# A graph network on one core: masks behind the picks, row numbers once a turn, and one arrival count for eight tiles

## What is computed

```python
def spmm(h):
    msg = h[src] * edge_w[:, None]
    agg = jax.ops.segment_sum(msg, dst, num_segments=N)
    return agg + self_w[:, None] * h
h = relu(batchnorm(spmm(x @ W1 + b1)))
x = layernorm(x + spmm(h @ W2 + b2))
# second layer: attention along the edges, softmax over edges of the same src ("row")
scores = (q[row] . k[col]) / sqrt(16) + edge_emb @ eb_w.T + eb_b
attn = softmax of scores over the edges of a row
out = segment_sum(attn * v[col], row);  x = layernorm(x + out @ out_w.T + out_b)
```

## Time and profile before

| | |
|---|---|
| median of 3 runs | 9340.04 us |
| profiled execution | 9334.91 us, its span 9333.3 us |
| mean granted TensorE clock | 0.796 of full |
| busy: TensorE matmul, weight load | 6708.6 us (72%), 5384.7 us (58%) |
| busy: VectorE, POOL, ScalarE | 5772.2 us (62%), 6065.1 us (65%), 2627.6 us (28%) |
| stretches in steady state | first product 600 to 2200 us, second product 2800 to 5200 us, expansion 5600 to 7400 us |

### The profile page before, as it was taken

How to read it: one execution, slowest core, us unless ns; L and a number is a source line. 1 busy time by engine, 2 the same in 40 slices (tenths; PEclk the granted TensorE clock), 3 DMA queues, 4 the chain that set the end, 5 groups by cost and what they waited for, 6 DMA issues and landing times. The chain is left out here.

```text
span 9333.3 us, 196145 instructions
## 1 busy us (share of the span) xinstructions
PE 6708.6 (72%) x37588; PEld 5384.7 (58%) x37589; DVE 5772.2 (62%) x15905; ACT 2627.6 (28%) x9043; POOL 6065.1 (65%) x6650
## 2 busy tenths in 40 slices
PE   6688888888677777777777646666666658854774
PEld 5556565656466766666666524444444447754663
DVE  7544444445466666666666565555555558888887
ACT  7311111111223333333333110000000025535884
POOL 6477777777655555555555657777777767744665
PEclk8688888898667677767677677878878789987997
DMA  1233333344321111111111133333333356643663
GB/s 45 57 105 107 107 106 108 108 110 109 94 75 42 42 42 42 42 41 41 40 40 39 46 98 114 114 113 114 114 113 114 114 156 167 168 107 103 165 164 96
DMA packets 1043673, 868.47 MB, mean 93 GB/s; under 512 B 188168, under 2 KB 936312, under 8 KB 1043624
## 3 DMA queue, kind: packets, MB, share of 16 engines
q0 software_dynamic: 179664, 437.87, 15.3%
q1 hardware_dynamic: 643032, 319.49, 13.1%
q10 hardware_dynamic: 220928, 110.57, 4.1%
HBM read 578.04 MB, written 287.84 MB: 93 GB/s over the span
## 5 line engine op out<-in xcount | busy, mean ns | idle before, releaser
L1561 POOL DMA_INDIRECT spmm_rows<-h_table,spmm_index_ring x3136 | 3120.1, 995 | 1738.7 <-issue 862.8
L1640 PE MATMUL bank<-spmm_rows,spmm_hot 128*128 x6660 | 1808.6, 365 | 145.5 <-SPq L1536 94.8
L1919 POOL DMA_INDIRECT kv_sorted<-expand_payload,expand_where_ring x1568 | 1503.5, 959 | 498.4 <-issue 398.3
L1640 PEld LDWEIGHTS bank<-spmm_rows,spmm_hot 128*128 128x128 f32 x6660 | 1404.2, 253 | 584.3 <-issue 564.2
L1612 DVE TENSOR_TENSOR region_ab<-region_ab,bank 128x128 f32 x3330 | 957.0, 287 | 1204.8 <-PE bank L1640 808.4
L1940 PE MATMUL bank<-region_ab,expand_hot_t 128*128 x3336 | 1117.2, 493 | 733.7 <-DVE expand_hot_t L1957 732.9
L1974 DVE SCALAR_TENSOR_TENSOR expand_payload<-expand_payload,region_c,bank 128x256 f32 x1668 | 801.1, 480 | 878.4 <-SPq L1881 620.2
L1940 PEld LDWEIGHTS bank<-region_ab,expand_hot_t 128*128 128x128 f32 x3336 | 765.5, 240 | 942.7 <-issue 817.1
L845 ACT COPY spmm_beside_next_slot<-bank 128x98 f32<-128x98 f32 x1568 | 377.6, 241 | 1903.3 <-PE bank L808 1895.8
L808 PE MATMUL bank<-spmm_beside_hot_hi,spmm_beside_hot_lo 128*128 128x98 bf16 x1568 | 556.3, 355 | 481.6 <-issue 481.6
L518 PE MATMUL bank<-spmm_beside_upto,spmm_beside_highs 128*98 128x128 bf16 x1568 | 686.3, 438 | 254.8 <-issue 252.0
(11 more groups left out here) (358 smaller groups left out, 11797.0 us busy)
## 6 DMA issues: line engine op xcount, KB each, us to landing
score_k_rows<-kv_sorted SPq DMA_DIRECT2D x420, 288.0 KB
mix_mixed<-kv_sorted SPq DMA_DIRECT2D x420, 256.0 KB
spmm_beside_attr_sb<-in_edge_attr_dram ACTq DMA_DIRECT2D x390, 256.0 KB
spmm_rows<-h_table,spmm_index_ring POOLq DMA_INDIRECT x3136
kv_sorted<-expand_payload,expand_where_ring POOLq DMA_INDIRECT x1568
kv_sorted<-spmm_beside_blank SPq DMA_DIRECT2D x1, 15232.0 KB
kv_sorted<-spmm_beside_blank SPq DMA_DIRECT2D x98, 136.0 KB
h_table<-region_ab SPq DMA_DIRECT2D x28, 448.0 KB, 3.0
```

Of the source, the lines that this page charges most:

```text
L1561: nc.gpsimd.indirect_dma_start(rows[:, k, :], None, table, bass.IndirectOffsetOnAxis(ap=index_ring[:, h, k % HALF:k % HALF + 1], axis=0)). ...
L1640: last = nc.tensor.matmul(sums_of(k), hot[:, k // HOTS % HOT_GROUPS, k % HOTS, :], tile_of(rows, place[k % HALF]), start=True, stop=True)
L1919: nc.gpsimd.indirect_dma_start(kv_sorted, bass.IndirectOffsetOnAxis(ap=where_ring[:, h, k % HALF:k % HALF + 1], axis=0), payload[:, k, 0:R ...
```

## The change

- `find_bases` writes one count per half (the count of its eighth tile) as a 32-bit integer in place of one per tile as 16-bit.
- `slots_of_half` reads eight places and that one count, masked to 11 bits. TensorE in both products uses it at column 0 of a half, now behind `work.tensor_step`, and waits for `arrived` once a half. VectorE in the expansion uses it once per eight tiles and waits for `freed` once.
- `Ranks.keep_earlier` for pair u+2 is called right behind the picks of pair u; the first two masks are made ahead of the loop.
- `RankBySource` works out row numbers once a turn, 16 at a time.
- VectorE in the products reads node numbers behind `work.vector_step` of column 0.

The same class `Ranks` serves a sort by destination that runs only for unsorted input, which this is not.

```diff
@@ -27,6 +27,7 @@
+S_HALVES = S_TILES // HALF
@@ -50,7 +51,7 @@
 assert N_CHUNKS * CHUNK == NT and N_CHUNKS % 2 == 0 and NT % 2 == 0
 assert 0 < LAST_TILES <= HALF and NT == E_TURNS
 assert W_BLOCKS * WINDOWS == S_TILES and CHUNK_TILES * CHUNKS == S_TILES and LAST_COLS % TURN == 0
-assert SRC_BLOCKS * SRC_WINDOWS == E_COLS
+assert SRC_BLOCKS * SRC_WINDOWS == E_COLS and E_COLS < 2048
 FULL_TURNS = LAST_COLS // TURN
@@ -144,8 +145,8 @@
         sum_place = sb("sum_place", [1, NT], I32)
         node_rows = sb("node_rows", [PLACE_ROW + 1, S_TILES], I32)
         node_d, node_s = node_rows[0:1, :], node_rows[S_ROW:S_ROW + 1, :]
-        until_wide, window_place = node_rows[UNTIL_ROW:UNTIL_ROW + 1, :], node_rows[PLACE_ROW:PLACE_ROW + 1, :]
-        until_window = until_wide.bitcast(U16)[:, 0:S_TILES]
+        until_row, window_place = node_rows[UNTIL_ROW:UNTIL_ROW + 1, :], node_rows[PLACE_ROW:PLACE_ROW + 1, :]
+        until_half = until_row[:, 0:S_HALVES]
         somes_done = sb("somes_done", [1, E_SOMES], U16)
         fill_tile = sb("fill_tile", [1, NT], I32)
         unsorted = sb("unsorted", [1, 1], I32)
@@ -197,7 +198,7 @@
         breaks = region_c[:, 0:CHUNK_LEN // 2 + 1].bitcast(BF16)
-        node_at, steps_row = until_wide, node_d.bitcast(BF16)[:, 0:S_TILES]
+        node_at, steps_row = until_row, node_d.bitcast(BF16)[:, 0:S_TILES]
         sum_places = window_place
         def column(flat):
@@ -208,6 +209,12 @@
                                                                  skip_runtime_bounds_check_because=reason)
             assert len(values) == n
             return values
+
+        def slots_of_half(eng, q):
+
+            places = loaded(eng, window_place[:, bass.ds(q * HALF, HALF)], HALF, TURN, WINDOW_SLOT)
+            until, = loaded(eng, until_half[:, bass.ds(q, 1)], 1, E_COLS, CLAMPED)
+            return places, until & 2047
         with ExitStack() as ph:
             sem = ph.enter_context(phase_semaphores(nc))
@@ -743,6 +750,7 @@
                 self.one_hots(self.hot_lo, keys_lo, 0, 0, self.lows_ready)
                 self.one_hots(self.hot_hi, keys_hi, 0, 0, self.highs_ready)
                 self.keep_earlier(dve, 0, 0)
+                self.keep_earlier(dve, 1, 1)
             def vector_step(self, dve, i, k):
                 c, q = i * TURN + k, 2 * i + k // HALF
@@ -752,8 +760,6 @@
                 if k % HALF == 2:
                     need(dve, self.found, c - 2)
                     self.one_hots(self.hot_hi, keys_hi, q + 1, (k // HALF + 1) % 2, self.highs_ready)
-                if k % 2 == 0:
-                    self.keep_earlier(dve, i * (TURN // 2) + k // 2 + 1, k // 2 + 1)
             def found_at(self, k):
                 return self.found_in[k // 2 % 2][:, k % 2 * NT:(k % 2 + 1) * NT]
@@ -768,6 +774,7 @@
                                                           scale=1.0, scalar=0.0, op0=ALU.mult, op1=ALU.add,
                                                           accum_out=self.slot[:, h, m % HALF:m % HALF + 1])
                 last.then_inc(self.picked, 2)
+                self.keep_earlier(dve, i * (TURN // 2) + k // 2 + 2, k // 2 + 2)
             def turn_pair(self, pe, u, half, k):
@@ -852,13 +859,13 @@
         class RankBySource(Ranks):
-            CHAINED = 2 * 3
+            CHAINED = 3
             def __init__(self, sem, tmp):
                 super().__init__(sem, tmp, base_s, bank[4])
                 self.slot_step, self.filled, self.blank_ready, self.tail_filled, self.fill_go = (
                     sem(n) for n in ("slot_step", "filled", "blank_ready", "tail_filled", "fill_go"))
-                self.slot_i, self.row_i, self.tile_i = (tmp(n, [P, HALF], I32) for n in ("slot_i", "row_i", "tile_i"))
+                self.slot_i, self.row_i, self.tile_i = (tmp(n, [P, TURN], I32) for n in ("slot_i", "row_i", "tile_i"))
                 self.blank = tmp("blank", [P, ROW])
             def vector_start(self, dve):
@@ -871,18 +878,18 @@
             def vector_end_step(self, dve, i, k):
                 v, link = nc.vector, self.link
-                c, h = i * TURN + k, k // HALF
+                c = i * TURN + k
                 if k == 0:
                     link.turn(i * self.CHAINED)
                 if k % 2 == 1:
                     self.pick_pair(dve, i, k - 1)
-                if k % HALF < HALF - 1:
+                if k < TURN - 1:
                     return
                 dve.wait_ge(self.picked, c + 1)
-                link(v.tensor_copy(self.slot_i[:, :], self.slot[:, h, :]))
+                link(v.tensor_copy(self.slot_i[:, :], self.slot[:, :, :].rearrange("p h k -> p (h k)")))
                 link(v.tensor_single_scalar(self.tile_i[:, :], self.slot_i[:, :], P.bit_length() - 1, ALU.arith_shift_right))
                 link(v.tensor_single_scalar(self.row_i[:, :], self.slot_i[:, :], P - 1, ALU.bitwise_and))
-                v.scalar_tensor_tensor(where[:, bass.ds(i * TURN + h * HALF, HALF)], self.row_i[:, :], float(S_TILES), self.tile_i[:, :],
+                v.scalar_tensor_tensor(where[:, bass.ds(i * TURN, TURN)], self.row_i[:, :], float(S_TILES), self.tile_i[:, :],
                                        ALU.mult, ALU.add)
             def vector_end(self, dve):
@@ -1148,7 +1155,7 @@
                         link(v.memset(same_window[:, 0:1], 0.0))
                         link(v.tensor_tensor(same_window[:, 1:], window_bc[:, 1:], window_bc[:, 0:S_TILES - 1], ALU.is_equal))
                         until = slice(UNTIL_ROW, UNTIL_ROW + 1)
-                        link(v.tensor_scalar(until_window, window_bc[until, :], 1.0, float(E_COLS), ALU.add, ALU.min))
+                        link(v.tensor_scalar(until_half, window_bc[until, HALF - 1::HALF], 1.0, float(E_COLS), ALU.add, ALU.min))
                         link(v.tensor_copy(place_i[at, :], window_bc[at, :]))
                         link(v.tensor_single_scalar(place_i[at, :], place_i[at, :], TURN - 1, ALU.bitwise_and))
                         link(v.tensor_scalar(behind[at, :], window_bc[at, :], float(E_COLS), float(TURN), ALU.is_ge, ALU.mult))
@@ -1594,11 +1601,12 @@
                     def turn(i, edges=True, tiles=TURN):
                         for h in range(-(-tiles // HALF)):
-                            node = loaded(mybir.EngineType.DVE, node_d[0:1, bass.ds(i * TURN + h * HALF, HALF)], HALF, NT - 1, CLAMPED)
                             for k in range(h * HALF, min(tiles, (h + 1) * HALF)):
                                 t = i * TURN + k
                                 if edges:
                                     work.vector_step(dve, i, k)
+                                if k % HALF == 0:
+                                    node = loaded(mybir.EngineType.DVE, node_d[0:1, bass.ds(t, HALF)], HALF, NT - 1, CLAMPED)
                                 if k % HOTS == 1:
                                     one_hots(i * (TURN // HOTS) + k // HOTS + 1, k // HOTS + 1)
                                 if edges:
@@ -1626,17 +1634,15 @@
                     def turn(i, edges=True, tiles=TURN):
                         for k in range(tiles):
                             t = i * TURN + k
-                            if k % HALF == 0:
-                                some = bass.ds(t, HALF)
-                                place = loaded(mybir.EngineType.PE, window_place[:, some], HALF, TURN, WINDOW_SLOT)
-                                until = loaded(mybir.EngineType.PE, until_window[:, some], HALF, E_COLS, CLAMPED, least=1)
                             if edges:
                                 work.tensor_step(pe, i, k)
+                            if k % HALF == 0:
+                                place, until = slots_of_half(mybir.EngineType.PE, i * 2 + k // HALF)
+                                pe.wait_ge(arrived, until)
                             if k % HOTS == 0:
                                 pe.wait_ge(row_hot_ready, i * (TURN // HOTS) + k // HOTS + 1)
                             if k % SUMS == 0:
                                 need(pe, added, t - SUMS)
-                            pe.wait_ge(arrived, until[k % HALF])
                             last = nc.tensor.matmul(sums_of(k), hot[:, k // HOTS % HOT_GROUPS, k % HOTS, :], tile_of(rows, place[k % HALF]),
                                              start=True, stop=True)
                             if k % SUMS == SUMS - 1 or k == tiles - 1:
@@ -1960,14 +1966,13 @@
                     for j in range(groups):
                         g = i * GROUPS + j
                         one_hots(g + 1, (j + 1) % 2)
-                        some = bass.ds(i * TURN + j * GROUP, GROUP)
-                        place = loaded(mybir.EngineType.DVE, window_place[:, some], GROUP, TURN, WINDOW_SLOT)
-                        until = loaded(mybir.EngineType.DVE, until_window[:, some], GROUP, E_COLS, CLAMPED, least=1)
+                        if j % 2 == 0:
```

(5 more changed lines are left out.)

## The result

The changed kernel takes **8751.79 us** (median of 4 runs, 8744.93 to 8757.54) where the kernel before takes 9339.88 us beside it (median of 4): a ratio of **0.9371**, 95% interval 0.9355 to 0.9388. That is 588 us less. The forecast was 382 us less, 8958, in a range that ends at 8760: the direction was right, the size was not, and the time lies 8 us outside the range.

A forecast was written before the change was run, and what follows sets the result against it. POOL was taken to bound first product and expansion, TensorE the second product: 27.4 - 3.2 - 1.2 = 23.0 us a turn, plus 0.5; 3.9 less times 98 turns is 382 us, giving 8958 us, range 8760 to 9125.

The forecast's parts named there:

- What bounds the kernel: POOL's DMA issue paces first product and expansion; TensorE paces the second product at 27.4 us a turn.
- Part 1: Second product, TensorE reads 9 values a half, not 16: gap 2.43 to 0.8 us, saving 3.2 us a turn.
- Part 2: Second product, masks made right behind the picks: TensorE's 1.2 us a turn wait for masks goes.
- What is late next: the picks: Second product: with masks earlier, VectorE's picks come late next, some 4 to 5 us between halves.
- Part 3: VectorE, second product: row numbers once a turn save 1.0 us, node read 0.5; 20.8 us a turn becomes a floor.
- Part 4: One count per eight tiles, first product and expansion: ring slack covers it; cost taken as 0, 50 us kept for the range.
- starved rings: Rival: the coarse count makes fetching and consuming take turns in first product and expansion; 10016 us, chance 0.04.
- The Sum: Second product at today's clock mix: 23.5 us a turn, 3.9 less, times 98 turns: 382 us saved.
- the clock stays up: Rival: shorter gaps keep TensorE at 2.4 GHz in most of the second product; 21.3 us a turn, 8742 us, chance 0.17.
- TensorE slow throughout: Rival: second product at the lower clock throughout, or a new wait at picks; 25.2 us a turn, 9124 us, chance 0.17.
- a read costs by the instruction: Rival: read price ignores length, so the second product's gap stays; 1.7 us a turn saved, 9173 us, chance 0.07.
- no relief: Rival: masks wait on VectorE for L788's result and stall it by what is saved; 9340 us, chance 0.03.

The follow-up runs named there:

- b_reads: Kernel before with only the new register reads and waits (expansion too) and the node read's new place; 9290.25 us, ratio 0.9951.
- a_masks_back_2: Changed kernel with the masks put back behind L740, new reads and row numbers kept; 9130.11 us, ratio 0.9787 to the kernel before.
- b_rows: Kernel before with only the row numbers worked out once a turn; 9312.81 us, ratio 0.9971.
- a_filled_gap: Changed kernel plus four useless 512-column matmuls ahead of the register reads of each half in the second product; 8667.65 us, ratio 0.9287.
- a_vector_more: Changed kernel plus one unused VectorE compare of 1024 elements in each half of the second product; 8813.21 us, ratio 0.9436.
- RW: New reads and row numbers without the masks' move, the same run as a_masks_back_2; 9130 us.
- RM: Changed kernel with row numbers worked out twice a turn again, so new reads and masks together; 8858.73 us, ratio 0.9495.
- a_rows_back: Changed kernel with row numbers twice a turn, on another chip where the kernel before takes 10626.46 us; 10332.94 us, ratio 0.9724.

## Why the prediction was wrong in size

**What bounds the kernel: right as to the stages, wrong as to the second product.** The stages paced by POOL did not move. But "TensorE sets the pace: 21.3 us of work a turn and 6.1 us idle" read the loop between the two engines as one engine with idle time to be taken off. VectorE's own wait for TensorE, 5.1 us a turn, was in the same rows: when TensorE comes sooner, it meets masks that aren't ready (b_reads).

**Part 1: the size nearly right, the price by the wrong measure.** New gap forecast 0.8 us a half (0.5 to 2.0), measured 1.05, of which half is put down to arrivals; saved 1.4 where 1.6 was taken. The old gap was dear by the width of its counts (2.42 to 1.35 us by that alone), and "16 values cost more than twice 8" was this and not the number. "No row shows a read of a single value" was so of the rows chosen, but the trace of the kernel before had one, SyncE's, and the two prices of TensorE's reads in the row shown above:

```profile
L207 SPq TENSOR_LOAD <-fill_tile x66: 262/268/278, 2807.4 to 4684.4; - x66
```

The Trainium skill (DMA: Bandwidth & Descriptors, Latency and other measured facts) gives a register read a floor of about 600 ns. This row, 0.27 us, and TensorE's shortest, 0.30 us, lie below it, so as a floor it does not hold here; the reads of eight 32-bit values, 0.59 us, lie at it.

**Part 2: right in kind, wrong in size.** "The wait of 1.2 us a turn goes" was meant as the whole worth. It falls to 79.9/87.9 = 0.9 us only, but without the move there would be 210.1 us of it in 1900 (a_masks_back_2), 2.8 a turn. The move keeps away part of the wait that Part 1 makes, and that is worth 369 us where 1.2 x 98 = 118 were put down. "What is late next: the picks" is not shown as it stands: no wait of TensorE for the picks is in the list, only that for the masks behind them. VectorE's wait for TensorE at the picks fell from 397.5/87.6 = 4.5 to 97.6/87.9 = 1.1 us a turn, below the 2 that were named as a sign.

**Part 3: right in the main.** Four instructions once a turn; the four take 0.85 us with 16 elements (317 + 176 + 175 + 177 ns) where they took 0.74 with 8, a miss of 0.1 us a turn. VectorE busy fell from 1061.44/58.5 = 18.1 to 1289.46/75.4 = 17.1 us a turn; b_rows alone has 17.4, which with the gaps is near the forecast 1.0. That it is "hidden today" holds (26 us alone), and that it matters afterwards too (97 on top of the others). As a floor it was set a little too high: a_filled_gap, with the same work on VectorE, turns in 20.3 us, below the 20.8 worked out.

**Part 4: right.** The first product and the expansion stand. In 600:2200 POOL waits 41.3 us for TensorE where it waited 17.4, and its fetches are 1230 to 1233. In the expansion its wait for VectorE is 10.1 us in 1800 (5000:6800) where it was 26.8. The starved rings did not come about, though TensorE waits 87.3 us for arrivals in 1900 us of the second product.

**The Sum: the step that failed.** "At today's mix of clock levels: 27.4 - 3.2 - 1.2 = 23.0", plus 0.5. TensorE's work was held at 21.3 us a turn. It became 18.2 at the higher clock, a gain of 3.1 us that the sum put at nothing; the idle time fell by 3.0 where 3.9 had been forecast. 3.0 + 3.1 = 6.1 against 3.9 is 2.2 us a turn, 216 us of 98 turns, and the miss in the time was 206. Of the signs of being wrong that the prediction named, this one came: the granted clock left 0.65 to 0.8. **The rival "the clock stays up"** gave 21.3 us a turn and 8742, for 21.2 and 8752 measured, at a chance of 0.17. It was right that the clock rises and that this is a good part of the gain, though shorter gaps of the reads alone don't bring it (b_reads, 0.67). That its number came out to 10 us is luck in part: it took the clock at the upper level throughout, where 0.85 was granted, and VectorE at 20.8 us as the bound, where a_vector_more and a_filled_gap show that VectorE, the clock and POOL each have a share; at the upper level the turn is 20.3. The doubt set against it, that TensorE would idle a quarter of the time, was sound as to the level, and wrong in holding 0.70 for likelier. The first product, at 0.88 with TensorE idle 14% of the time, was the nearer example: the changed kernel too idles 14% (3.0 of 21.2). But the rows could not have settled it, for idle shares of 17% and 18% went with clocks of 0.67 (b_reads), 0.72 (RW) and 0.85 (RM). "TensorE slow throughout" (9124), "a read costs by the instruction" (9173) and "no relief" (9340) are out by the clock, the gap and the time, and "starved rings" by Part 4.

That the rise of the clock is a cause and no mere companion rests on the filled versions, which raise it and add work: 201 us on the kernel before, 84 on the one after. How the 588 us divide between clock and waits is not settled by these: the two parts of 3.0 and 3.1 us are bookkeeping, since a faster TensorE changes the waits and fewer waits the clock.

## What to carry to other kernels

Where two engines feed each other in a loop, an idle time of one is worth what is left when the other is asked to come earlier: take the stretch apart by who is waiting behind the gap, and expect edits that are worth little alone to be worth much together. Do not hold the clock at its present value when an edit removes idle time of TensorE: cost the work at both levels and let the range hold both, for here the idle share did not tell the clock. Look for the register reads' own rows before pricing them by what is idle. If a gap can't be removed, filling it with matmuls that nobody needs is a cheap thing to try, and it made both kernels faster.

## What was not expected of the hardware

- A register read of eight counts on TensorE took 1.92 us when they were 16-bit and 0.59 us when 32-bit, and the idle gap of two reads fell from 2.42 to 1.35 us; one 32-bit value took 0.27 to 0.30 us.
- At least 3.3 us of useless matmuls in each turn, which fell from 27.4 to 25.3 us, made the kernel 2.1% faster (clock 0.70 to 0.93).
- The granted clock fell to 0.67 with no gap over 2 us, where waits of 1.3 us on average stood (243.2/181) at the masks; two versions with 4.0 and 4.2 us of idle time a turn ran at 0.85 and 0.72.
- POOL's indirect DMA took 1037 ns on average with more work on VectorE (a_vector_more), 1026 in a_filled_gap and 997 with VectorE relieved beside the same filling.
- One chip took 14% longer for the same kernel (10626 against 9334 us); in the trace of a_rows_back there VectorE is held 96 times for 5.0 us in 1600 us of the first product.
